# Loops of eighteen supertiles and twenty chunks, loads split over two DMA queues, paired stores: a four-layer image kernel on one Trainium2 core

## The reference, cut to what matters

```python
x = x + layer0(_gn(x)); x = x + layer1(_gn(x)); x = x + layer2(_gn(x)); x = x + layer3(_gn(x))
# layer 0: every pixel's 3x3 neighbourhood (wrapped) is 3 tokens of 48 values
    x = _fold_to_kernels(in_x)
    x = x + attention(_ln(x)) @ w_attn_proj.T            # 4 heads of 12
    x = x + gelu(_ln(x) @ w_fc.T) @ w_fc_proj.T
    out = einsum(sum over the tokens of _ln(x), conv_w) + conv_b
# layer 1: 1x1 convolutions, 16 x 16; the gates divide by a channel's mean (out1) and maximum (out3)
    wh = conv1x1(out2 / (out1 + EPS), W2, b2); gray = conv1x1(out4 / (out3 + EPS), W3, b3)
    out = conv1x1(x * (1.0 + sigmoid(tanh(wh)) + sigmoid(tanh(gray))), W4, b4)
# layer 2: rational 3x3 convolution, for every output channel, input channel and tap
    P = sum(A[..., i] * x**i for i in range(6)); Q = 1.0 + abs(sum(Bc[..., i - 1] * x**i for i in range(1, 5)))
    out = sum of P / Q over input channels and taps
# layer 3: 3x3 B-spline convolution (8 bases) plus silu(x) through base weights
```

## Time and profile before

| | |
|---|---|
| median of 3 runs | 9667.91 us (9665.2 to 9704.05) |
| profiled execution, own time | 9659.51 us |
| its span, first to last instruction | 9657.6 us |
| busy in the span | PE 84%, DVE 81%, ACT 78%, POOL 64% |
| granted TensorE clock, mean | 0.948 |
| moved by DMA | 565 MB, mean 59 GB/s |

### The profile page before, as it was taken

The page is one execution under the profiler, slowest core; times in us unless marked ns, Lnnn a source line. Parts: engine busy times, 40 slices in busy tenths (PEclk is TensorE's granted clock), DMA queues, the critical chain, the costliest instruction groups (busy, mean ns, idle before and its releaser), DMA issues. The chain is left out here.

```text
span 9657.6 us, 141494 instructions
## 1 busy us (share of the span) xinstructions
PE 8079.0 (84%) x35042; PEld 2745.1 (28%) x35042; DVE 7784.3 (81%) x9341; ACT 7530.9 (78%) x8315; POOL 6169.8 (64%) x3354
## 2 busy tenths in 40 slices
PE   5999999999999999402998999899899899992799
PEld 2333333333333333100222222222222222220233
DVE  6777777777777776775999999899899999894787
ACT  4666666666666666365999999999999999992887
POOL 3555555555555554002999999999999999992111
PEclk9999999999999999756999999999999999996899
DMA  2000000000000000254333233323332233235555
GB/s 87 12 13 11 12 11 11 11 11 11 13 11 11 12 11 3 110 170 134 70 71 68 59 68 71 69 61 65 71 71 64 60 70 71 65 64 134 132 146 124
DMA packets 258449, 565.42 MB, mean 59 GB/s; under 512 B 71659, under 2 KB 179787, under 8 KB 244183
## 3 DMA queue, kind: packets, MB, share of 16 engines
q1 hardware_dynamic: 221746, 536.51, 22.6%
q0 software_dynamic: 35744, 17.87, 1.0%
HBM read 367.15 MB, written 186.72 MB: 57 GB/s over the span
## 5 line engine op out<-in xcount | busy, mean ns | idle before, releaser
L1226 POOL TENSOR_TENSOR l_a<-l_a 128x1018 f32<-128x1018 f32 x2117 | 3919.7, 1883 | 334.9 <-ACT l_a L1401 327.7
L1356 DVE TENSOR_TENSOR l_r<-l_pps,l_a 128x509 f32<-128x509 f32 x4234 | 2653.6, 680 | 377.7 <-PE l_pps L1239 311.3
L1401 ACT ACTIVATE l_a<-l_a 128x2036 f32<-128x2036 f32 x1194 | 2269.4, 1901 | 52.6 <-ACT l_a L1394 46.8
L1239 PE MATMUL l_qps<-l_mv,wst 123*128 123x509 bf16 x4248 | 1283.8, 384 | 754.8 <-DMA l_mv<-pw 408.3
L1394 ACT ACTIVATE l_a<-l_qps 128x1018 f32<-128x1018 f32 x1593 | 1604.1, 1016 | 172.5 <-PE l_qps L1239 145.8
L599 POOL TENSOR_TENSOR a_pr<-a_pr 128x768 f32<-128x768 f32 x384 | 896.5, 2335 | 807.9 <-DVE a_pr L537 792.0
L1239 PE MATMUL l_pps<-l_mv,wst 123*128 123x509 bf16 x4234 | 1334.8, 381 | 56.5 <-DVE l_r L1356 46.0
L675 ACT ACTIVATE a_g<-a_fps 128x512 f32<-128x512 f32 x1152 | 645.4, 595 | 755.7 <-PE a_fps L419 631.8
L1292 PE MATMUL l_aux<-l_r,l_sums 128*32 128x509 f32 x8448 | 1140.7, 606 | 0.5 <-issue 0.4
L1362 DVE TENSOR_SCALAR l_a<-l_qps 128x1018 int32<-128x1018 int32 x796 | 961.3, 1208 | 9.3 <-PE l_qps L1239 8.0
L537 DVE TENSOR_TENSOR a_pr<-a_qkv,a_at 128x768 f32<-128x768 f32 x576 | 854.8, 1536 | 2.2
(11 more groups left out here) (180 smaller groups left out, 11911.9 us busy)
## 6 DMA issues: line engine op xcount, KB each, us to landing
l_mv<-pw SPq DMA_DIRECT2D x1608, 79.5 KB
l_gx<-g SPq DMA_DIRECT2D x66, 1040.0 KB
l_sh<-planes SPq DMA_DIRECT2D x536, 127.2 KB, 6.2
planes<-l_s SPq DMA_DIRECT2D x66, 1018.0 KB, 4.6
a_xt<-g SPq DMA_DIRECT2D x192, 160.0 KB, 3.3
pw<-pw_hi SPq DMA_DIRECT2D x20, 1000.0 KB
pw<-pw_mid SPq DMA_DIRECT2D x20, 1000.0 KB
pw<-pw_lo SPq DMA_DIRECT2D x20, 1000.0 KB
```

What stands on the lines that cost most here:

```text
L1226: g.tensor_tensor(a, a, a, ALU.mult).then_inc(sq_p, 1)
L1239: return t.matmul(out, wst[:, k, n * P:(n + 1) * P], x[:, n // NPP, cols], start=True, stop=True)
L1356: v.tensor_tensor(to, pps[:, (2 * m + h) % P_BANKS, 0:SUB], pair_of(A, m)[:, h, :], ALU.mult).then_inc(mul_done, 1)
L1401: s_.activation(a, a, ACT.Abs_reciprocal_sqrt, bias=1.0).then_inc(root_done, GROUP)
```

## The change

Six edits:

1. The loop bodies grow. In layer 0 a body holds `ROUNDS` = 20 chunks, so the loop has 3 rounds. In layer 2 a body holds 18 supertiles, so 3 rounds, and the remaining 12 supertiles follow in straight code. SP's loop in layer 2 keeps 6 supertiles.
2. norm0's loads and stores alternate between SP's queue and ACT's queue.
3. Layer 1's loads are split over both queues. The image is walked along its rows, in runs of 16 adjacent words, and only G is read one word in every 128; a maximum per row is taken of each piece as it comes, and a last one over the 1,024 row maxima. The first add waits for both halves of x, the bias and G's first piece.
4. powers stores two chunks with one DMA: rows of 3,200 bytes, two double-chunk slots in place of three single ones. hi and lo stay on SP's queue, mid is issued by ACT.
5. The three rows of ones in mv are loaded from DRAM (written in layer 1) in place of the fills. PE's wait on `c_in` becomes 80: the two constants and the ones of all three slots.
6. Layer 3's front: Y is issued by ACT with five slots, x and the weights by SP, the weights after x; they are prepared after the seventh piece; half of G's stores go from ACT's queue.

```diff
-BODY = 6
+BODY, QUEUED = 18, 6
@@ run_steps
         for s in range(LAG_LATE, LAG_LATE + STEPS):
             step(it, s)
+    for s in range(LAG_LATE, LAG_LATE + NSUP % BODY * NSUB * NPAIR2):
+        step(NSUP // BODY, s)
@@ steps (layer 0)
-    with engine.Fori(0, (LEAD_OUT - LEAD_IN) // TURNS) as thrice:
-        for i in range(TURNS):
-            body(Plan(thrice * TURNS + (LEAD_IN + i), (LEAD_IN + i) % TURNS, LEAD_IN))
+    with engine.Fori(0, (LEAD_OUT - LEAD_IN) // ROUNDS) as again:
+        for i in range(ROUNDS):
+            body(Plan(again * ROUNDS + (LEAD_IN + i), (LEAD_IN + i) % TURNS, LEAD_IN))
@@ norm0
-                for k in range(4):
-                    sp.dma_start(X[:, k * HW // 4:(k + 1) * HW // 4], x[:, k * HW // 4:(k + 1) * HW // 4]).then_inc(x_in[k], 16)
+                for k in (0, 2):
+                    load(sp, k)
...
+                for k in (1, 3):
+                    load(act, k)
                 norm.scalar_part(act)
+                for k in range(1, W // COLS, 2):
+                    store(act, k)
@@ layer1
+            def load(e, half):
+                rows = slice(half * HW // 2, (half + 1) * HW // 2)
+                e.dma_start(X[:, rows], x[:, rows]).then_inc(x_in[0], 16)
+                for k in range(half, LOADS, 2):
+                    n = HW // LOADS
+                    e.dma_start(G[:, k * n:(k + 1) * n], x1[:, k * n:(k + 1) * n]).then_inc(x_in[k], 16)
...
-                            link(v.scalar_tensor_tensor(image[:, at, :], laid[:, at, :], shift0[:], image[:, at, :], ALU.add, ALU.add))
+                            e.wait_ge(x_in[j], 16 if j else 64)
+                            link(v.scalar_tensor_tensor(image[:, :, at], laid[:, :, at], shift0[:], image[:, :, at], ALU.add, ALU.add))
+                            v.tensor_reduce(tops[:, j, :], image[:, :, at], AX.X, ALU.max)
...
-                    link(v.reduce_max(top[:, 0:1], X[:], AX.X))
+                    link(v.reduce_max(top[:, 0:1], tops[:].rearrange("p k h -> p (k h)"), AX.X))
@@ powers
-    BUF = 3
-    CH = 800
+    CH, SLOTS2 = 800, 2
...
+                for q in range(NPAIRS):
+                    at, n = span(q)
+                    done = min(2 * q + 2, len(chunks))
+                    for m, t, ready in ((0, hi, hi_ready), (2, lo, lo_ready)):
+                        sp.wait_ge(ready, done * DEG)
+                        sp.dma_start(lines[m, :, :, :, at:at + n], t[:, q % SLOTS2, :, 0:n]).then_inc(stored[q % SLOTS2], 16)
...
+                    if k % 2 or k == len(chunks) - 1:
+                        q = k // 2
+                        first, cols = span(q)
+                        act.wait_ge(mid_ready, (k + 1) * DEG)
+                        act.dma_start(lines[1, :, :, :, first:first + cols], mid[:, q % SLOTS2, :, 0:cols]).then_inc(stored[q % SLOTS2], 16)
@@ layer2
                 for g in range(SLOTS):
-                    sp.wait_ge(mv_cleared, g + 1)
                     load_supertile(g, g)
+                    sp.dma_start(mv[KROWS - 3:KROWS, g].rearrange("p c n -> p (c n)"), ones).then_inc(c_in, 16)
+                    if g == 0:
+                        sp.dma_start(sums[:], l2w[0]).then_inc(c_in, 16)
+                        sp.dma_start(pick[:], l2w[1]).then_inc(c_in, 16)
...
-                pe.wait_ge(c_in, 32)
+                pe.wait_ge(c_in, 80)
...
-                for u in range(SLOTS):
-                    v.memset(mv[:, u], 1.0).then_inc(mv_cleared, 1)
@@ layer3
+            YSLOTS = 5
...
+            def store(e, half):
+                for k in range(PIECES):
+                    e.wait_ge(g_ready, k + 1)
...
+                    for j in range(half * QUAD // 2, (half + 1) * QUAD // 2):
...
-                        if p == 3:
+                        if p == 6:
...
+                    for k in range(PIECES):
+                        if k >= YSLOTS:
+                            act.wait_ge(added, k - YSLOTS + 1)
...
+                        act.dma_start(Y[:, k % YSLOTS, :], rows).then_inc(x_in[k], 16)
                     norm.scalar_part(act)
+                    store(act, 1)
```

More of the change, by code:

```diff
@@ L207, in _ @@
             def _(sp):
-                for k in range(4):
-                    sp.dma_start(X[:, k * HW // 4:(k + 1) * HW // 4], x[:, k * HW // 4:(k + 1) * HW // 4]).then_inc(x_in[k], 16)
+                for k in (0, 2):
+                    load(sp, k)
                 norm.sync_part(sp, pair)
[L211 to L214, removed]
+                for k in range(0, W // COLS, 2):
+                    store(sp, k)
                 sp.wait_ge(edges, 2)
@@ L717, in _, with layer1 @@
                 steps(act, body)
-def layer1(nc, x, x1, bias0, x2, pair, w1, raw2, pieces, wst, pw):
+def layer1(nc, x, x1, bias0, x2, pair, w1, raw2, pieces, ones, wst, pw):
     TILE = 1024
@@ L747, in layer1 @@
             top = sb1("l1_top", [P, 8])
+            tops = sb1("l1_tops", [P, LOADS, H])
+            one = sb1("l1_one", [ONES, SUB], BF16)
             stat = sb1("l1_stat", [P, 8])
@@ L784, in _ @@
                     sp.dma_start(rest2[:], raw2).then_inc(raw_in, 16)
[L785 to L790, removed]
+                    sp.dma_start(shift0[:], bias0).then_inc(x_in[0], 16)
+                    load(sp, 0)
                     norm.sync_part(sp, pair)
@@ L798, in _ @@
                         sp.dma_start(flat, part2[:, m, :]).then_inc(stored, 16)
+                    sp.wait_ge(one_made, 1)
+                    sp.dma_start(ones.rearrange("r n -> (r n)").rearrange("(p n) -> p n", p=ONES), one[:]).then_inc(stored, 16)
                     for k in range(4):
@@ L922, in _ @@
                     s = nc.scalar
+                    load(act, 1)
                     norm.scalar_part(act)
@@ L951, in powers @@
     STORES = 3 * 16
+    NPAIRS = (len(chunks) + 1) // 2
     with ExitStack() as ctx2:
@@ L969, in powers @@
         wst_in = sem("pw_wst_in")
-        stored = [sem(f"pw_stored{u}") for u in range(BUF)]
+        stored = [sem(f"pw_stored{u}") for u in range(SLOTS2)]
         def power(k, i):
@@ L975, in power, with piece, span, wait_stored @@
             return up[:, k % 2, i - 1, 0:n] if i else GP[:, at:at + n]
+        def piece(t, k, i):
+            return t[:, k // 2 % SLOTS2, i, k % 2 * CH:k % 2 * CH + chunks[k][1]]
+        lines = pw.rearrange("t c i (b n) -> t b c i n", b=NB)
+        def span(q):
+            return chunks[2 * q][0], sum(n for _, n in chunks[2 * q:2 * q + 2])
+        def wait_stored(e, q):
+            e.wait_ge(stored[q % SLOTS2], (q // SLOTS2 + 1) * STORES)
         with nc.Block() as block:
@@ L992, in _ @@
                 sp.wait_ge(wst_in, (len(A_PARTS) + 3) * 16)
-                for u in range(BUF):
-                    sp.wait_ge(stored[u], len(chunks[u::BUF]) * STORES)
+                for q in range(NPAIRS - SLOTS2, NPAIRS):
+                    wait_stored(sp, q)
             @block.vector
```

130 lines of the change are left out of this document (59 added, 71 removed).

## The result

The changed kernel takes 9626.8 us (median of 6 runs, 9621.0 to 9636.4), the kernel before 9689.5 (6 runs, 9665.2 to 9704.1): a ratio of 0.994 with a 95% interval of 0.9922 to 0.9957. It is faster by 63 us of 9,690 in the medians (42 to 76 us by the interval), clear of the noise though small, and not by the 108 us of the sum. The profiled executions stand at 9621.0 and 9659.5 us, 38.5 us apart.

The account below looks back on a forecast made before the run. No engine bounds the whole span, so stages were priced alone (ACT paces layer 2). Terms -50 - 50 + 5 - 13 - 17 + 20 - 3 = -108 us, giving 9551.5 or 9560; forecast 9555, range 9495 to 9605.

Parts of the forecast that it names:

- powers: Stage storing hi, mid and lo: two-chunk stores with mid issued by ACT give net -17 us, bounds -44 to +9.
- size of a chunk: In the powers stage, time per chunk falls from 17.07 to 15.8 us, 26 us less over 20 chunks.
- late first store: In the powers stage, the first store must wait for chunk 1's hi: 9 us later, with empty queues.
- ACT's time to issue: In the powers stage, ACT issues 11 stores; its idle 16 us a pair covers an issue up to that length.
- The rival to which I gave 3%: In powers, wider rows on two queues hinder each other: 24.1 us a chunk, +148 us, total 9729; chance 3%.
- Two double slots suffice: In powers, while one pair's 6.1 MB drain in 31 us, DVE needs only 21.4 and ACT 18.
- Start of layer 2: PE waits for slot 2's ones, issued after all 72 loads: +20 us, bounds +4 to +21.
- The loops: Layers 0 and 2: fewer jumps back save 50 us each; bounds for both together 95 to 104.
- Layer 1: Shorter strides speed adds and statistics, the maximum is spread, the first add starts 3 us later: net -13, bounds -23 to -5.
- The first norm: norm0: with two queues the first piece lands later, delaying everything behind DVE: +5 us, bounds 0 to +5.
- layer 3's front: Y's landing unchanged, weights' preparation partly uncovered +4, G's stores -7: net -3 us, bounds -35 to +9.
- The base: Starting time of the whole kernel for the sum: profiled execution 9659.5 us, or median of three runs 9667.9.

Follow-up runs that it names:

- the split pair: Changed kernel with all powers stores on SP's queue, ones first, norm0 on one queue, and the first two chunks stored singly: 9537.4 us, ratio 0.9881.
- single stores: Changed kernel with powers as before the change (single chunks, three slots, all stores on SP's queue): 9586.2 us, ratio 0.9898.
- narrow rows: Changed kernel with each two-chunk store of powers split in two of 800 columns (1,600-byte rows), slots and queues kept: 9602.3 us, executed once.

## Why the prediction was wrong, and where it was right

**The step that failed is powers**, 46 us of it: -17 forecast, +28.8 measured. Its size of a chunk was right (15.8 forecast, 15.65 measured), its 9 us for the late first store too (9.3 and, by the split pair, 10.7), but both hold for pairs on one queue: with these the stage gains 15 us, the forecast's 17. What failed is that the prediction charged the second queue with nothing but ACT's time to issue, and held that time to be covered. The issues were indeed cheap (a median of 0.62 us), but the queue itself cost 44 us (405.0 against 361.0), a term that stood nowhere in the sum. The rule of the Trainium skill ("DMA: Bandwidth & Descriptors", Issuing engines are not separate DMA queues), that a second issuing engine only saves time to issue, agrees with the trace for rows of 1,600 bytes (377.2 against 375.5 us). For rows of 3,200 bytes the trace disagrees: 405.0 against 361.0, and the measurement decides. The rival to which I gave 3%, wide rows on two queues in each other's way, named the place and the combination; its price of 24.1 us a chunk was too high: the stage's 44 us over 21 chunks are 2.1 a chunk on top of 15.65. Its picture, every engine busy and each slower, is only half of it: the median packet is as quick as on one queue (132 against 133 ns), a few are far slower, and the share of the DMA engines falls to 0.37 at worst.

**"Two double slots suffice"** holds for one queue: on one queue the pairs step by 31.3 us, the time in which they drain, as the prediction had it; with two queues and 560 columns a third slot gave nothing.

**Start of layer 2**: the mechanism was right, the term was mis-sized by 9 us. PE started 54.2 us after the first load, not 44.5, because the 72 loads took 52.5 us to land and not 43.0. The 1,440 packets of 4,072 bytes took 278 ns on average in the kernel before and 340 in the changed one; 291 with single stores, 318 with these on two queues, 337 with pairs on one queue, 342 with narrow rows, and 302 behind the changed kernel's own paired stores when the ones are issued first. So neither the pairs nor the width of their rows explains it, and why these loads are slower stays open. Issuing the ones first wins back 30 us.

**The loops** were right to 2 us each, in the changed kernel and alone. By the price of a compare-and-branch in the Trainium skill ("Advanced Engine Details and Errata", Control Flow Timing), about 108 ns, the estimate for all 20 jumps is 2 us; 104.5 us were measured.

**Layer 1** was right to 2 us and in its parts (add 3.67 against 3.7, statistic 0.68 against 0.64, first add about 6 us late instead of 3). **The first norm** came out at +4.8 for +5, **layer 3's front** at -4.0 for -3: stores -8.7 for -7, while the weights' preparation lost its cover.

**The base.** I set the sum against one profiled execution of 9659.5 us and a median of three, 9667.9. Six runs put the median at 9689.5, and two profiles of the kernel before differ by 19 us in the spline stage alone. In the profiles this eats 18 us of the gain; in the medians it doesn't (-62.7 us, ratio 0.994). The sum of 108 less 46 for powers and 9 for the start of layer 2 is 53 us, near what the medians show. Of the 72 us between 9555 and 9626.8, 55 are these two terms and 26 are the base (about 9663 was taken where six runs gave 9689.5); the other parts came out some 4 us better than forecast, and 6 us are the difference between profiles and medians. Without the miss at powers the median would be near 9581, inside the range.

**Still open**: why a packet of 3,200 bytes takes up to 728 ns when two queues are served, and what an engine does then. Each transfer had 640 rows in all kernels, so its size changed with the width of its rows, and the runs can't tell the two apart. That uneven engines hold the slots is read from the packets in flight; no run took it away alone.

## What to carry to other kernels

Change the size of the transfers and the queue that issues them one at a time: here the first gained 15 us and both together lost 29. When a wait guards several loads, issue the small ones ahead of the large ones, or the engine waits for the last of the queue. Before a sum of small terms is set against a profile, ask how far one stage varies from execution to execution; here the spline stage alone spread over 60 us.

## What the runs showed of the hardware that was not expected

- Rows of 3,200 bytes move at 198 GB/s on one queue and, with a third of them on a second queue, at 174 (182 where it is the high piece, over the steady part); rows of 2,240 bytes at 190 and 182; rows of 1,600 bytes at 181 either way.
- Where they run in full, the stores keep 0.51 to 0.53 of the DMA engines busy on one queue and on two, and less (down to 0.37) where wide rows on two queues thin out: the second queue opened no idle engine.
- A program's last stage, fed by small loads from POOL's queue, varied from 713 to 773 us with the same instructions and the same busy times of ACT (586 to 587 us).
